# Rotary attention: where the two table products, the exchange of rows and the sum are made

## The chip, the cores and the metric

One core of a Trainium2 chip runs the whole program in one launch. The metric is the device time of one execution, in microseconds (us), as the median of three runs. The traces and pages are those of one profiled execution. Engines: TensorE (PE; PEld is its weight load), VectorE (DVE), ScalarE (ACT), GpSimd (POOL), SyncE (SP; SPq is its queue of DMA issues).

## The reference

The program is a chain of eight blocks over x of 8 x 512 x 256. Only the sixth is touched, a causal attention of 16 heads of 64 with rotary positions and four learned keys and values ahead of the tokens:

```python
def rotate_half(x):
    x1 = x[..., ::2]; x2 = x[..., 1::2]
    return jnp.stack((-x2, x1), axis=-1).reshape(x.shape)
def apply_rope(t):
    ...
    return t * cos + rotate_half(t) * sin
h = rms_norm(x, norm_weight)
q, k, v = jnp.split(h @ w_qkv.T, 3, axis=-1)        # then split into 16 heads
q = apply_rope(q); k = apply_rope(k)
k = jnp.concatenate([pm, k], axis=2); v = jnp.concatenate([pm, v], axis=2)
scores = jnp.einsum('bhid,bhjd->bhij', q, k) * scale
scores = jnp.where(causal, scores, jnp.finfo(scores.dtype).min)
out = jnp.einsum('bhij,bhjd->bhid', jax.nn.softmax(scores, axis=-1), v)
return out.transpose(0, 2, 1, 3).reshape(b, n, heads * dim_head) @ w_out.T
```

## The kernel before

`attention_core` serves two stages; with `rope` set it is the rotary attention, without it another block's attention (the `flat_` branches), which the diff leaves alone. Tensors lie with features on the partitions: a pair of heads fills 128 partitions, 512 tokens lie along a row. Values of 32 bits are split into a high and a low half of 16 bits, so that a product is three matmuls.

**Slots.** Work goes by a pair of heads n of a batch, 8 pairs and 8 batches. `slots` runs the slots -2, -1 and 0 once and then 64 slots in a loop of four turns of 16. In slot s each engine works on up to four pairs at once, in an order written out by hand in its `rope_slot`: the rotation of pair s+2, the scores and maxima of pair s+1, the transposed scores and exponentials of pair s, and the value products and outputs of pair s-1. Every eighth slot also projects a batch's outputs (`outputs`, line 915, and `add_outputs`, line 1028). Engines meet through semaphores only. A wait holds everything behind it on its engine, the queue of DMA issues included.

**The rotation.** Operation j is pair j//2, its queries when j is even and its keys when odd. All of them use one PSUM bank (`pj`), one pair of SBUF tiles (`ab`) and one tile for the sum (`rot`), so they go one after the other:

- TensorE's `project` (line 832) makes `pj`, once `evac` says that it is free.
- VectorE's `rotate` multiplies `pj` by the cosines into `ab[:,0]` (line 979) and copies `pj` with neighbouring partitions exchanged into `ab[:,1]` (line 980, STREAM_SHUFFLE). It first waits for the sum of the operation before.
- GpSimd's `turn` multiplies `ab[:,1]` by the signed sines (line 1138), and `sum_up` adds both into `rot` (line 1142).
- ScalarE's `high` casts `rot` to 16 bits into `QK` (line 1080), and GpSimd's `low` subtracts to get the low half (line 1147). The next sum waits for it.

**The order around it.** VectorE's slot: low weights of the second tile (`low_weights`, line 1007) and maxima of the third group (line 990); the split of the maxima; low weights of the third and fourth tile; rotate the queries; `normalise` (reciprocal, line 1019, which waits for the last value product, `pv_done`); `low_values` (line 1014); maxima of the first group; rotate the keys; maxima of the second group (lines 990, 991); `low_outputs` (line 1024); low weights of the first tile. TensorE's slot: project the queries; transposed scores 3 of pair s-1 (lines 881 to 888); value products (line 901), the last of which counts `pv_done`; transposed scores 0; scores of the first group (line 857); project the keys; turn the outputs; scores of the second group; transposed scores 1; scores of the third group, which wait for the maxima of the second; project values (line 838); transposed scores 2. ScalarE's slot: exponentials 2 and 3 of pair s-1 (lines 1088, 1093); cast of the keys of pair s+1; the turned maxima (line 1083); high values (line 1098); exponentials 0; copy of the outputs (line 1101); exponentials 1; cast of the queries of pair s+2. SyncE's slot, once each of 64: wait for this slot's last value product, then load 2 KB of value tails for a later pair (line 1064).

Of the kernel before, what the change touches and what calls it, by code (L numbers as in the profile page):

```python
# [5 lines left out]
P=128  # L6
# [754 lines left out]
def attention_core(nc, XT, HT, c_):  # L761
# [26 lines left out]
    with ExitStack() as ctx:  # L788
# [5 lines left out]
        QK=sb("QK",[P,4,2,2,PM+T],F16)  # L794
        ab=sb("ab",[P,2,T]) if rope else None
        rot=sb("rot",[P,1 if rope else 2,T])
        PH=sb("PH",[P,2,PCOLS],F16); PL=sb("PL",[P,2,PCOLS],F16); P32=sb("P32",[P,2,2,PM+T])
# [5 lines left out]
        mtp=s_ps[:,0,:].bitcast(BF16)  # L803
        h_hi,h_ready,cleared,proj,evac,turned,summed,hi,lo,pm_kept=[sem(n) for n in "h_hi,h_ready,cleared,proj,evac,turned,summed,hi,lo,pm_kept".split(",")]
        v_done,v_hi,v_low,o_low=[sem(n) for n in "v_done,v_hi,v_low,o_low".split(",")]
        tail_in=[sem(f"tail_in{i}") for i in range(4)] if rope else None
        s_done,maxed,m_step,m_ready,m_turned,m_copied=[sem(n) for n in "s_done,maxed,m_step,m_ready,m_turned,m_copied".split(",")]
# [5 lines left out]
        def batch(it,n): return (it*BPI+n//NP_)%NB  # L813
# [149 lines left out]
        def _(dve):  # L963
# [10 lines left out]
            def rotate(it,j):  # L974
                n,what=divmod(j,2)
                if rope:
                    if j: dve.wait_ge(summed,it*2*S+j)
                    dve.wait_ge(proj,it*2*S+j+1)
                    nc.vector.tensor_tensor(ab[:,0],pj[:,:],c_.tab[:,0],ALU.mult)
                    nc.vector.stream_shuffle(ab[:,1],pj[:,:],[i^1 for i in range(32)]).then_inc(evac,1)  # L980
                else:
# [76 lines left out]
        if rope:  # L1058
            @block.sync
            def _(sp):  # L1060
                sp.wait_ge(cleared,CL)
                def tail_rows(b,n):
                    rows=c_.tails[bass.ds(b,1),:,n%NP_].rearrange("a m part h d -> (a m) part h d")
                    sp.dma_start(V[0:PM,n%4,QT,:,:,0:DH],rows).then_inc(tail_in[n%4],16)
                for n in range(4): tail_rows(0,n)
                with loop(nc,sp,NB//BPI) as it:
                    for n in range(4,S+4):
                        sp.wait_ge(pv_done,it*S*QT+(n-3)*QT)
                        tail_rows(batch(it,n),n)
                for i in range(4): sp.wait_ge(tail_in[i],16*(NB*NP_//4+1))  # L1070
        else: c_.select(nc,block,ctx,hi)
        @block.scalar
        def _(act):
# [35 lines left out]
            def rope_slot(it,s):  # L1109
# [4 lines left out]
                if s>=-1: high_values(it,s+1)  # L1114
                if s>=0: exps(it,s,0)
                if s>=1: keep_outputs(it,s-1)
                if s>=0: exps(it,s,1)
                high(it,2*(s+2))
            def flat_slot(it,s):
# [15 lines left out]
        def _(pool):  # L1135
            def turn(it,j):
                pool.wait_ge(evac,it*2*S+j+1)
                nc.gpsimd.tensor_tensor(ab[:,1],ab[:,1],c_.tab[:,1],ALU.mult).then_inc(turned,1)  # L1138
            def sum_up(it,j):
                if j: pool.wait_ge(lo,it*2*S+j)  # L1140
                pool.wait_ge(turned,it*2*S+j+1)
                nc.gpsimd.tensor_tensor(rot_of(j),ab[:,0],ab[:,1],ALU.add).then_inc(summed,1)  # L1142
            def low(it,j):
# [10 lines left out]
            def rope_slot(it,s):  # L1154
                q,k=2*(s+2),2*(s+2)+1
                if s>=-1: low(it,2*(s+1)+1)
                turn(it,q); sum_up(it,q)
                if new_batch(s): low_tokens(it,s+3)
                turn(it,k)
                low(it,q)  # L1160
                sum_up(it,k)
# [112 lines left out]
def rope_table():  # L1274
# [3 lines left out]
    f=np.repeat(f,2,axis=-1).T  # L1278
    sign=np.where(np.arange(DH)%2==0,-1,1).astype(np.float32)[:,None]
    one=np.stack([np.cos(f),np.sin(f)*sign],1).astype(np.float32)  # L1280
# [986 lines left out]
```

## Time and profile before

| | |
|---|---|
| median of three runs | 3782.42 us (3779.88 to 3782.56) |
| profiled execution | 3805.44 us |
| its span, first to last instruction | 3803.5 us |
| attention core | from about 2081 to 3021 us of the span |
| busy over the span | PE 83%, DVE 59%, ACT 44%, POOL 32% |

The page cuts the span into 40 slices and gives each engine's busy share in tenths, and the TensorE clock that the throttle granted, in tenths of full speed. Attention fills slices 22 to 31 or so:

```profile
## 2 busy tenths in 40 slices
PE   8677488988889889689985899999999889999571
...
DVE  4667644444444444478865888889888745555233
ACT  2179333333333333366743555556555534444230
POOL 0032410000000000133311655566555544443342
PEclk9899755555555555599997999999999955555786
DMA  4011110000000000011001000000000010110335
```

Times in the rows below are in us from the span's start unless marked ns. "[0.34 <-POOL att_rot L1142]" behind a row of a timeline says that the engine was idle for 0.34 us ahead of it and what ended that. The rows are of the profiled execution; a term taken from them is set against its time, 3805.4 us.

### The profile page before, as it was taken

Reading aid. Unit: us, or ns where it says so; the run is one execution under the profiler, and the core shown is the slowest. Engines: PE = TensorE matmul, PEld = TensorE weight load, DVE = VectorE, ACT = ScalarE, POOL = GpSimd, SP = SyncE. Lnnn points to the kernel's source line nnn. Section 1 sums busy time; section 2 is a strip of 40 time slices with the busy share of each in tenths; the row PEclk is TensorE's granted clock in tenths of the full one; section 3 lists DMA queues with packets and bytes.
Section 4 is the critical chain, followed back from the end, with each engine's and each line's share of the span. In section 5 each row is a group of like instructions: output and inputs, shape, how many; then the busy total and the mean of one; then the engine's idle time right before and its main releaser. Section 6 shows DMA issues by size and latency. Waiting matters only on the chain. (4 is left out here: it accounts for less than half of the span.)

```text
span 3803.5 us, 143700 instructions
## 1 busy us (share of the span) xinstructions
PE 3140.8 (83%) x58958; PEld 2400.2 (63%) x58958; DVE 2247.7 (59%) x6777; ACT 1692.0 (44%) x5164; POOL 1216.8 (32%) x1533
## 2 busy tenths in 40 slices
PE   8677488988889889689985899999999889999571
PEld 5545278888888888545532666666666567777451
DVE  4667644444444444478865888889888745555233
ACT  2179333333333333366743555556555534444230
POOL 0032410000000000133311655566555544443342
PEclk9899755555555555599997999999999955555786
DMA  4011110000000000011001000000000010110335
GB/s 133 1 55 46 31 26 14 14 25 14 25 14 14 25 14 25 15 33 25 17 1 52 2 2 3 2 3 3 2 3 2 16 51 30 32 33 28 109 102 173
DMA packets 110725, 116.07 MB, mean 31 GB/s; under 512 B 52782, under 2 KB 94199, under 8 KB 110112
## 3 DMA queue, kind: packets, MB, share of 16 engines
q1 hardware_dynamic: 102416, 87.33, 8.1%
q0 software_dynamic: 7824, 21.46, 1.6%
q8 instruction: 403, 6.60, 0.7%
q14 instruction: 82, 0.67, 0.1%
HBM read 79.62 MB, written 29.13 MB: 29 GB/s over the span
## 5 line engine op out<-in xcount | busy, mean ns | idle before, releaser
L676 PE MATMUL banks<-hp,whp 128*128 128x8 f16 x24576 | 741.6, 168 | 117.5 <-DVE hp L743 117.5
L676 PEld LDWEIGHTS banks<-hp,whp 128*128 128x128 f16 x24576 | 698.0, 104 | 178.2 <-DVE hp L743 169.4
L709 ACT ACTIVATE ig<-banks 128x32 f32<-128x32 f32 x512 | 100.9, 197 | 577.2 <-PE banks L676 577.2
L738 DVE SCALAR_TENSOR_TENSOR carry<-ig 128x16 f32<-128x16 f32 x512 | 91.6, 179 | 424.9 <-ACT ig L709 424.9
L646 POOL COPY HT<-hist 128x128 f32 x64 | 21.2, 407 | 986.6 <-DVE hp L748 986.6
L1088 ACT ACTIVATE att_PH<-att_stp 128x1024 f16<-128x1024 f32 (+3 forms) x258 | 183.2, 710 | 325.4 <-PE att_stp L888 325.4
L1753 PE MATMUL rnn_banks<-rnn_hp,rnn_whp 128*128 128x8 f16 x6144 | 285.4, 171 | 40.3 <-ACT rnn_hp L1811 15.4
L1753 PEld LDWEIGHTS rnn_banks<-rnn_hp,rnn_whp 128*128 128x128 f16 x6144 | 248.3, 107 | 107.1 <-ACT rnn_hp L1811 76.1
L1007 DVE TENSOR_TENSOR att_PL<-att_P,att_PH 128x1024 f16<-128x1024 f32 (+3 forms) x257 | 266.3, 1075 | 0.5 <-issue 0.2
L654 PE MATMUL banks<-xs,wxp 128*128 128x64 f16 x3168 | 263.7, 241 | 0.0
L1147 POOL TENSOR_TENSOR att_QK<-att_rot,att_QK 128x512 f16<-128x512 f32 x133 | 174.2, 1310 | 239.6 <-ACT att_QK L1080 239.6
L1905 DVE TENSOR_TENSOR rnn_hp<-rnn_hist,rnn_hp 128x16 f16<-128x16 f32 x512 | 97.7, 191 | 227.6 <-ACT rnn_hist L1812 218.7
L1811 ACT ACTIVATE rnn_hp<-rnn_banks 128x16 f16<-128x16 f32 x512 | 93.7, 183 | 279.5 <-PE rnn_banks L1753 277.4
L832 PE MATMUL att_pj<-att_hT,att_w 128*128 128x512 f16 x804 | 201.0, 386 | 17.4 <-POOL att_hT L1151 15.6
L990 DVE TENSOR_REDUCE att_mx<-att_sp 128x2 f32<-128x264 f32 (+3 forms) x263 | 209.6, 818 | 1.1 <-PE att_sp L862 1.1
L1138 POOL TENSOR_TENSOR att_ab<-att_ab,att_rope 128x512 f32<-128x512 f32 x134 | 169.8, 1267 | 124.2 <-DVE att_ab L980 123.4
L1142 POOL TENSOR_TENSOR att_rot<-att_ab 128x512 f32<-128x512 f32 x134 | 204.2, 1524 | 14.8
L654 PEld LDWEIGHTS banks<-xs,wxp 128*128 128x128 f16 x3168 | 194.5, 126 | 0.0
L1093 ACT ACTIVATE att_P<-att_stp 128x1024 f32<-128x1024 f32 (+3 forms) x258 | 180.6, 700 | 5.3 <-DVE att_PL L1007 5.3
L901 PE MATMUL att_acc<-att_V,att_PH 128*128 128x65 f16 (+1 forms) x3584 | 180.0, 193 | 0.0
L743 DVE TENSOR_TENSOR hp<-og,tc 128x16 f16<-128x16 f32 x512 | 90.1, 176 | 144.2 <-ACT tc L715 144.2
L901 PE MATMUL att_acc<-att_V,att_PL 128*128 128x65 f16 x1792 | 175.0, 192 | 0.0
(606 smaller groups left out, 7712.9 us busy)
## 6 DMA issues: line engine op xcount, KB each, us to landing
gen_w<-in_L_cond_W_dram SPq DMA_DIRECT2D x32, 512.0 KB
exp_xt<-expert_rows_scratch SPq DMA_DIRECT2D x80, 129.0 KB
edge_cb<-cols_scratch SPq DMA_DIRECT2D x16, 512.0 KB, 3.8
XT<-expert_found_scratch SPq DMA_DIRECT2D x16, 512.0 KB, 4.9
mod_xn<-in_x_dram SPq DMA_DIRECT2D x8, 512.0 KB
XT<-in_xT_dram SPq DMA_DIRECT2D x1, 4096.0 KB
out_dram<-exp_ob SPq DMA_DIRECT2D x64, 64.0 KB, 2.2
attw_st<-in_L_attn_w_qkvT_dram SPq DMA_DIRECT2D x6, 512.0 KB
```

What stands on the lines that cost most here:

```text
L654: last=nc.tensor.matmul(out, wxp[:,wpart,k,col:col+128], xs[:,st,xpart,k,steps], start=False,stop=False,skip_group_check=True)
L676: last=nc.tensor.matmul(out, whp[:,wpart,k,col:col+128], hp[:,k,hpart], start=False,stop=True,skip_group_check=True)
L832: last=nc.tensor.matmul(pj[:,:],c_.w_of(n)[:,wpart,k,col:col+P],h_of(n)[:,xpart,k,PM:PM+T],start=(i==0),stop=(i==5)); i+=1
L901: last=nc.tensor.matmul(out[:,0:wide],p[:,h,at:at+P],V[:,n%4,tt,part,h,0:wide],start=(tt==0 and a==0 and p is PH and part==0),stop=(tt==(R ...
L990: i=nc.vector.tensor_reduce(out=mx[:,:,qt:qt+1],in_=s_ps[:,:,at:at+w_],axis=X_AX,op=ALU.max); at+=w_
L1007: i=nc.vector.tensor_tensor(PL[:,:,at:at+w_],P32[:,t%2,:,0:w_],PH[:,:,at:at+w_],ALU.subtract)
L1088: nc.scalar.activation(PH[:,:,at:at+w_],st_ps[:,:,0:w_],ACT.Exp,scale=DH**-0.5)
L1093: i=nc.scalar.activation(P32[:,t%2,:,0:w_],st_ps[:,:,0:w_],ACT.Exp,scale=DH**-0.5)
L1138: nc.gpsimd.tensor_tensor(ab[:,1],ab[:,1],c_.tab[:,1],ALU.mult).then_inc(turned,1)
L1142: nc.gpsimd.tensor_tensor(rot_of(j),ab[:,0],ab[:,1],ALU.add).then_inc(summed,1)
L1147: nc.gpsimd.tensor_tensor(dst[:,1],rot_of(j),dst[:,0],ALU.subtract).then_inc(lo,1)
L1753: last=nc.tensor.matmul(pre(st,par)[:,u,j], whp[:,wpart,k,u*P:u*P+P], hp[:,k,hpart], start=False,stop=True,skip_group_check=True)
```

## The change

The exchange of neighbouring rows moves behind the product with the sines. VectorE makes both products from `pj`; in the second, the row's own sine is used with the sign of the row that it will go to (the table's signs are flipped). Two DMAs on SyncE's queue, one for the odd and one for the even rows, copy `ab[:,1]` into a new tile `swapped` with neighbours exchanged, 64 rows of 2 KB each. GpSimd's `turn` goes, and its `sum_up` waits for both DMAs. SyncE's slot becomes: the wait for the last value product and the tail load as before, then the swap of the queries, then that of the keys. ScalarE casts the queries ahead of the outputs' copy and of exponentials 1, in place of behind them. GpSimd's order is otherwise kept.

```diff
@@ attention_core
+        swapped=sb("swapped",[P,T]) if rope else None
...
+        swapped_in=sem("swapped_in")
@@ VectorE, rotate
                     nc.vector.tensor_tensor(ab[:,0],pj[:,:],c_.tab[:,0],ALU.mult)
-                    nc.vector.stream_shuffle(ab[:,1],pj[:,:],[i^1 for i in range(32)]).then_inc(evac,1)
+                    nc.vector.tensor_tensor(ab[:,1],pj[:,:],c_.tab[:,1],ALU.mult).then_inc(evac,1)
@@ SyncE
+                def swap_rows(it,j):
+                    sp.wait_ge(evac,it*2*S+j+1)
+                    for r in range(2): sp.dma_start(swapped[r::2,:],ab[1-r::2,1]).then_inc(swapped_in,16)
+                def rope_slot(it,s):
+                    if s>=1:
+                        sp.wait_ge(pv_done,it*S*QT+s*QT)
+                        tail_rows(batch(it,s+3),s+3)
+                    swap_rows(it,2*(s+2))
+                    swap_rows(it,2*(s+2)+1)
                 for n in range(4): tail_rows(0,n)
-                with loop(nc,sp,NB//BPI) as it:
-                    for n in range(4,S+4):
-                        sp.wait_ge(pv_done,it*S*QT+(n-3)*QT)
-                        tail_rows(batch(it,n),n)
+                slots(rope_slot,sp)
@@ ScalarE, rope_slot
                 if s>=0: exps(it,s,0)
+                high(it,2*(s+2))
                 if s>=1: keep_outputs(it,s-1)
                 if s>=0: exps(it,s,1)
-                high(it,2*(s+2))
@@ GpSimd
-            def turn(it,j):
-                pool.wait_ge(evac,it*2*S+j+1)
-                nc.gpsimd.tensor_tensor(ab[:,1],ab[:,1],c_.tab[:,1],ALU.mult).then_inc(turned,1)
             def sum_up(it,j):
                 if j: pool.wait_ge(lo,it*2*S+j)
-                pool.wait_ge(turned,it*2*S+j+1)
-                nc.gpsimd.tensor_tensor(rot_of(j),ab[:,0],ab[:,1],ALU.add).then_inc(summed,1)
+                pool.wait_ge(swapped_in,32*(it*2*S+j+1))
+                nc.gpsimd.tensor_tensor(rot_of(j),ab[:,0],swapped[:,:],ALU.add).then_inc(summed,1)
@@ GpSimd, rope_slot
-                turn(it,q); sum_up(it,q)
+                sum_up(it,q)
                 if new_batch(s): low_tokens(it,s+3)
-                turn(it,k)
                 low(it,q)
                 sum_up(it,k)
@@ rope_table
-    sign=np.where(np.arange(DH)%2==0,-1,1).astype(np.float32)[:,None]
+    sign=np.where(np.arange(DH)%2==0,1,-1).astype(np.float32)[:,None]
```

## Rows read from the trace of the kernel before

**Rows 1.** Windows view, one ordinary slot; columns as the first row names them:
```profile
...
core 0: us, PE busy (x) PEld busy (x) DVE busy (x) ACT busy (x) POOL busy (x), PEclk, DMA share, GB/s
...
2602.90:2615.80 12.90, 11.92 (x221) 8.44 (x218) 12.24 (x24) 8.14 (x17) 8.18 (x7) 1.00 0.01 3
...
```

**Rows 2.** Waits of VectorE from 2100 to 3000 us: us in total, times, longest:
```profile
...
DVE att_inv L1019 <- PE att_acc L901: 12.5, 42, 0.3
DVE att_ab L979 <- PE att_pj L832: 10.5, 35, 2.6
DVE att_ab L979 <- POOL att_rot L1142: 9.6, 21, 0.8
...
```

**Rows 3.** Timeline of VectorE: start us, us, engine, line, op, out<-in, [idle before]:
```profile
...
2500.79 0.72 DVE L980 STREAM_SHUFFLE att_ab<-att_pj 128x512 f32<-128x512 f32 x1
2501.58 0.21 DVE L1019 RECIPROCAL att_inv<-att_acc 128x8 f32<-128x8 f32 x1
...
2504.40 0.69 DVE L979 TENSOR_TENSOR att_ab<-att_pj,att_rope 128x512 f32<-128x512 f32 x1 [0.34 <-POOL att_rot L1142]
...
2506.50 0.16 DVE L991 TENSOR_REDUCE att_mx<-att_sp 128x2 f32<-128x8 f32 x1
...
2512.96 0.67 DVE L979 TENSOR_TENSOR att_ab<-att_pj,att_rope 128x512 f32<-128x512 f32 x1
...
2514.60 0.21 DVE L1019 RECIPROCAL att_inv<-att_acc 128x8 f32<-128x8 f32 x1 [0.30 <-PE att_acc L901]
...
2517.32 0.69 DVE L979 TENSOR_TENSOR att_ab<-att_pj,att_rope 128x512 f32<-128x512 f32 x1
...
```

**Rows 4.** Timeline of TensorE, from the key rotation of one slot to the next:
```profile
...
2506.72 0.39 PE L857 MATMUL att_sp<-att_QK 64*128 64x512 f16 x2 [0.94 <-DVE att_mx L991]
...
2515.81 1.47 PE L832 MATMUL att_pj<-att_hT,att_w 128*128 128x512 f16 x6
...
```

**Rows 5.** Timeline of GpSimd, the sums of queries and of keys in one slot:
```profile
...
2503.01 1.27 POOL L1142 TENSOR_TENSOR att_rot<-att_ab 128x512 f32<-128x512 f32 x1
...
2509.48 1.87 POOL L1142 TENSOR_TENSOR att_rot<-att_ab 128x512 f32<-128x512 f32 x1
...
```

**Rows 6.** Groups by shape, 2100 to 3000 us: xcount, busy us, mean ns, idle before:
```profile
...
L1138 POOL TENSOR_TENSOR att_ab<-att_ab,att_rope 128x512 f32<-128x512 f32 x126 | 159.7, 1267 | 113.4 <-DVE att_ab L980 112.6
L1007 DVE TENSOR_TENSOR att_PL<-att_P,att_PH 128x776 f16<-128x776 f32 x63 | 114.2, 1813 | 0.5 <-issue 0.2
...
L980 DVE STREAM_SHUFFLE att_ab<-att_pj 128x512 f32<-128x512 f32 x127 | 92.2, 726 | 0.0
L979 DVE TENSOR_TENSOR att_ab<-att_pj,att_rope 128x512 f32<-128x512 f32 x127 | 86.6, 682 | 20.2 <-PE att_pj L832 10.5 <-POOL att_rot L1142 9.6
...
```

**Rows 7.** Timeline of the SyncE queue, the tail load of the slot at 2500 us:
```profile
...
2501.71 0.26 SPq L1064 DMA_DIRECT2D att_V<-value_tails_scratch  x1
```

**Rows 8.** The instructions of line 1064: duration ns min/median/max:
```profile
...
L1064 SPq DMA_DIRECT2D att_V<-value_tails_scratch x68: 254/255/301, 2075.0 to 3013.5; - x68
L1064 SPq FUSED_REGOPS  x64: 37/37/101, 2117.5 to 3013.4; - x64
L1064 SPq MOVE att_V<-value_tails_scratch x64: 29/29/29, 2117.6 to 3013.5; - x64
...
```

**Rows 9.** The stores of line 2010, 64 KB each: issue, and issue to landing:
```profile
...
L2010 SPq DMA_DIRECT2D out_dram<-exp_ob x64: 315/426/510, 3756.2 to 3800.3; - x64
...
DMA to landing us min/median/max: 1.9/2.2/4.2
```

**Rows 10.** The page, DMA issues: count, KB each, median us to landing:
```profile
...
XT<-expert_found_scratch SPq DMA_DIRECT2D x16, 512.0 KB, 4.9
...
```

**Rows 11.** Timeline of ScalarE, the first and second tile's exponentials:
```profile
...
2503.53 1.02 ACT L1093 ACTIVATE att_P<-att_stp 128x1024 f32<-128x1024 f32 x1
...
2505.83 0.82 ACT L1088 ACTIVATE att_PH<-att_stp 128x776 f16<-128x776 f32 x1 [0.50 <-PE att_stp L888]
...
```

**Rows 12.** Timeline of VectorE in a batch slot, behind the output products:
```profile
...
2456.68 0.96 DVE L1007 TENSOR_TENSOR att_PL<-att_P,att_PH 128x776 f16<-128x776 f32 x1
...
```

More of the change, by code:

```diff
@@ L803, in attention_core @@
         mtp=s_ps[:,0,:].bitcast(BF16)
-        h_hi,h_ready,cleared,proj,evac,turned,summed,hi,lo,pm_kept=[sem(n) for n in "h_hi,h_ready,cleared,proj,evac,turned,summed,hi,lo,pm_kept".split(",")]
+        h_hi,h_ready,cleared,proj,evac,summed,hi,lo,pm_kept=[sem(n) for n in "h_hi,h_ready,cleared,proj,evac,summed,hi,lo,pm_kept".split(",")]
         v_done,v_hi,v_low,o_low=[sem(n) for n in "v_done,v_hi,v_low,o_low".split(",")]
+        swapped_in=sem("swapped_in")
         tail_in=[sem(f"tail_in{i}") for i in range(4)] if rope else None
```

## The prediction

> **What bounds the kernel now.** I went from the stage to the loop inside it. The attention stage repeats one slot per pair of heads: 64 in the loop, 56 ordinary ones and eight that also project a batch's outputs. The windows view of one ordinary slot, 12.90 us long, has TensorE busy 11.92 us and VectorE 12.24 us at a granted clock of 1.00, the 2.4 GHz level [rows 1]. Both look full, so busy shares don't say which is the bound; the waits do. In 42 of 62 slots VectorE's reciprocal waits for the last value product of TensorE, and its rotation of the keys (line 979, second use in a slot) waits 35 times for TensorE's projection and 21 times for GpSimd's sum [rows 2]. So VectorE has slack in most slots, 0.3 us at one place and 0.2 us at the other, and TensorE doesn't.
>
> The two timelines give the loop. VectorE begins the keys' rotation at 2504.40 and ends the maxima of the second group at 2506.66, that is 2.26 us later [rows 3]. TensorE, which had waited 0.94 us for exactly this, starts the third group's scores at 2506.72 [rows 4]. It works through the slot's list until the last value product, which releases the reciprocal at 2514.60, 7.94 us after the maxima [rows 3]. Then it makes the next transposed scores, the first scores and the keys' projection, which ends at 2515.81 + 1.47 = 2517.28 [rows 4], and the next rotation of the keys starts at 2517.32, 2.72 us after the reciprocal [rows 3]. 2.26 + 7.94 + 2.72 = 12.92 us is the slot. A delay between the reciprocal and the keys' rotation is paid in full; work taken off VectorE elsewhere isn't.
>
> In that last piece a second chain runs beside TensorE: query products, GpSimd's turn, GpSimd's sum, key rotation. It is just long enough to show. In the slot at 2500 the queries' shuffle ends at 2501.51, the sum at 2503.01 + 1.27 = 2504.28, and the keys' rotation starts at 2504.40, after 0.34 us of waiting [rows 3, 5]; the piece is 2.82 us there. Over the stage the piece is about 2.77 us. This second chain is what the change touches.
>
> **The change part by part.** *VectorE.* The shuffle (726 ns) becomes a product with one PSUM and one SBUF operand, as line 979 is (682 ns) [rows 6]. In the loop this is 0.04 us per slot, 64 x 0.04 = 2.8 us gained.
>
> *GpSimd* loses its turns, 1.27 us each, one before each sum [rows 6]. Of its remaining work only the queries' sum, 1.27 us, stands on the chain [rows 5].
>
> *SyncE and DMA.* Each rotation now issues two DMAs of 64 rows of 2 KB. For the queries SyncE comes to them only behind this slot's wait for the last value product and the load of value tails: the program has that wait first. In the next slot the queries' rotation starts at 2512.96 and its two operations of 0.7 us are done by 2514.3, while the value product releases the reciprocal only at 2514.60 [rows 3]: the products are ready, and the queue isn't. Working from the reciprocal's start (2501.58), SyncE begins the tail load at +0.13 and has issued it at +0.39 [rows 3, 7]. Its register work before an issue is 37 + 29 ns [rows 8], so the first swap is issued at +0.46.
>
> The time from the first issue to the landing of both has no row of its own. The second issue follows by one issue's length: 0.26 us for the tail load [rows 8], 0.43 for a 64 KB store [rows 9]; I take 0.3, nearer the first, since the swap's rows are as plain as a load's. For the landing the nearest row is the 64 KB store of 64 rows, 1.9 us at least, 2.2 in the median, 4.2 at most [rows 9]. Those are issued eight in a row onto each other's heels, while attention's DMA share is 0.01 [rows 1], so I take its least, 1.9. That makes 2.2 us from first issue to both landed. The bounds: 1.3 us, if a landing into SBUF takes half of that store's; and, on the line from 64 KB in 2.2 us to 512 KB in 4.9 us [rows 10], 3.35 us for the 256 KB of both.
>
> The Trainium skill, "DMA: Bandwidth & Descriptors", section on the anatomy of one DMA, puts a DMA at about 2.0 us fixed plus bytes over 436 GB/s. For 128 KB that is an estimate of 2.3 us in place of 1.9, and by it the sum below would be 26 us longer. It adds that the wait is mostly the target memory's receipt, HBM's being the heaviest, which speaks for less with SBUF as the target; no row here shows an SBUF to SBUF transfer.
>
> Then GpSimd wakes (0.10, estimated by VectorE's 0.12 after GpSimd), sums (1.27), and VectorE starts 0.12 later: 0.46 + 2.2 + 0.10 + 1.27 + 0.12 = 4.15 us from the reciprocal to the keys' rotation, in place of 2.77. **+1.38 us per slot.** The batch slots have the same piece, and behind it TensorE's output products wait for VectorE as the scores do, so I count all 64 slots, once each, as the tail load's 64 register steps count them [rows 8]: 64 x 1.38 = 88 us.
>
> For the keys, SyncE is free: it issues right behind the products, at +1.4 us from the rotation's start, the rows land at +3.6, and the sum is made by +5.3 even if GpSimd first waits for a subtraction of VectorE's. The next to ask for it is the next slot's query rotation, which started at 2512.96, 8.6 us after the keys' at 2504.40 [rows 3]. So it costs nothing; were SyncE 3 us late, it would begin to.
>
> *ScalarE.* The queries' cast moves ahead of the outputs' copy and the second exponentials. ScalarE ends the first tile at 2504.55, +2.97, and the sum is there at +4.0: it stands idle for a microsecond, and the second exponentials, which began at 2505.83, +4.25, begin about as much later [rows 11]. That delays no one, since TensorE's use of them, in the transposed scores behind the third group's, has itself moved by 1.38. If that cover were gone, a good microsecond could stand on the loop instead.
>
> *Prologue.* Six rotations ahead of the loop have the transfer in series too, at most 0.9 us each (2.2 for a turn of 1.27); I take 3 us, which cancels VectorE's gain of 2.8.
>
> **Sum:** +88 us. The profiled execution took 3805.4 us and the median of the three runs is 3782.4, 0.6% less; the difference is not in this stage's terms, so I add 88 to either: 3893 for a profiled one, **3870 for the median**.
>
> **Rivals.** *A short swap.* Landing 1.3 us after the first issue: the piece is 3.25 us, +0.48 per slot, +31: 3813 us. For it: a quiet DMA system, a target in SBUF. Against: no row below 1.9.
>
> *A long swap.* At 3.35 us (two transfers behind each other) +2.53 per slot, +162: 3944 us. For: 4.9 us for 512 KB. Against: those are large loads issued together.
>
> *Not slower: the swap is hidden and VectorE gets its time back.* The place is the lock-step of the key sum and the subtraction of line 1007. The 128x776 subtraction takes 1813 ns in the mean beside GpSimd [rows 6], and 0.96 us in a batch slot [rows 12]; GpSimd's sum takes 1.87 us there in place of 1.27 [rows 5]. So 0.85 us per ordinary slot is lost on VectorE to GpSimd. If VectorE were the bound and the sum came after the subtraction, 56 x 0.85 = 48 us would be won: 3735 us. It decides only if the swap lands within 0.8 us of its issue (4.15 - 2.2 + 0.8 = 2.75), and even then TensorE holds the slot at 12.9, which leaves about 5 us: 3777, no change. The Trainium skill, "SBUF — State Buffer", section on its two sides, states this lock for a VectorE operation with two SBUF inputs against a GpSimd one that reads SBUF, and that the first to start makes the other wait; the rows agree.
>
> *The clock.* TensorE's busy share falls from 92% to some 84%. If a tenth of the slots fell to the 1.2 GHz level, about 6 x 11.9 = 71 us would come on top: 3941. Nothing in this stage's rows shows it.
>
> **Chances.** My forecast (swap of 1.9 to 2.7 us, 3850 to 3902) 0.75; short swap 0.10; long swap 0.08; clock 0.03; hidden swap 0.04, half of it faster and half no change. The range reaches 3815 at the short swap and 3920 toward the long one; outside are the hidden one, half of the short, most of the long and the clock, near 0.2. This kernel's measurement can tell 0.2% (7.6 us) from no change: faster 0.02, within 0.02, slower 0.96.
>
> **What would show it.** In the changed profile: slots near 14.3 us; the keys' rotation waiting 1.3 us or more for GpSimd's sum in nearly every slot and never for the projection; TensorE's wait ahead of the third group's scores up from 0.94 to about 2.3 us; the first swap issued right behind each tail load, not right behind the queries' products; ScalarE idle ahead of the queries' cast. I am wrong if the swaps are issued ahead of the tail load's wait, if they land within 0.8 us, or if the slot stays at 12.9.

## The result, and the profile after

The changed kernel takes 3977.9 us (median of 4 runs, 3973.7 to 3979.2) against 3781.2 us (4 runs): ratio 1.052, interval 1.050 to 1.0537, or 197 us slower. The forecast was 3870, range 3815 to 3920: the sign was right, the size less than half. The profiled execution's span is 3976.2 us, where the kernel before had 3803.5.

VectorE's timeline of the changed kernel, two slots in a row, answers to [rows 3] (line 1021 is the reciprocal, 981 the rotation's first product, 993 the end of a group's maxima):

```profile
2542.40 0.18 DVE L1021 RECIPROCAL att_inv<-att_acc 128x8 f32<-128x8 f32 x1
...
2546.78 0.69 DVE L981 TENSOR_TENSOR att_ab<-att_pj,att_rope 128x512 f32<-128x512 f32 x1 [1.93 <-POOL att_rot L1147]
...
2548.86 0.16 DVE L993 TENSOR_REDUCE att_mx<-att_sp 128x2 f32<-128x8 f32 x1
...
2558.50 0.21 DVE L1021 RECIPROCAL att_inv<-att_acc 128x8 f32<-128x8 f32 x1 [0.37 <-PE att_acc L903]
...
2563.07 0.69 DVE L981 TENSOR_TENSOR att_ab<-att_pj,att_rope 128x512 f32<-128x512 f32 x1 [2.09 <-POOL att_rot L1147]
...
2565.15 0.16 DVE L993 TENSOR_REDUCE att_mx<-att_sp 128x2 f32<-128x8 f32 x1
...
2573.24 0.21 DVE L1021 RECIPROCAL att_inv<-att_acc 128x8 f32<-128x8 f32 x1 [0.37 <-PE att_acc L903]
```

Reciprocal to the keys' rotation takes 4.38 and 4.57 us, where it took 2.82. And the stretch that the forecast left alone, from the end of the second maxima to the next reciprocal, takes 2573.24 - 2565.31 = 7.93 us in the second slot, as before, but 2558.50 - 2549.02 = 9.48 us in the first. The windows view over that first slot says why (columns as in [rows 1]; the seventh figure, behind POOL's, is the granted clock):

```profile
2544.00:2546.00 2.00, 2.00 (x25) 1.21 (x24) 0.86 (x2) 1.18 (x2) 0.61 (x1) 1.00 0.28 105
2546.00:2548.00 2.00, 0.41 (x10) 0.19 (x4) 1.22 (x3) 1.30 (x3) 1.26 (x2) 1.00 0.00 0
2548.00:2550.00 2.00, 0.77 (x12) 0.54 (x12) 2.00 (x5) 1.22 (x2) 0.56 (x1) 1.00 0.23 88
2550.00:2552.00 2.00, 2.00 (x22) 1.83 (x20) 2.00 (x3) 0.00 (x0) 1.22 (x1) 0.59 0.14 51
2552.00:2554.00 2.00, 2.00 (x19) 1.04 (x17) 1.30 (x4) 0.53 (x2) 0.74 (x1) 0.56 0.00 0
2554.00:2556.00 2.00, 2.00 (x43) 1.25 (x42) 0.70 (x1) 0.93 (x5) 0.00 (x0) 1.00 0.00 0
```

TensorE is busy for 0.41 and 0.77 of 2.00 us in two windows, and in the next two its clock is 0.59 and 0.56: most of that time is at 1.2 GHz. TensorE's timeline around it, to be held against [rows 4]:

```profile
2549.08 0.39 PE L859 MATMUL att_sp<-att_QK 64*128 64x512 f16 x2 [2.66 <-DVE att_mx L993]
...
2550.27 2.07 PE L840 MATMUL att_vo<-att_w,att_hT 128*128 128x128 f16 x18
```

The wait ahead of the third group's scores is 2.66 us, where it was 0.94. The 18 products of line 840 behind it take 2.07 us; in a slot of the same run in which the clock doesn't fall they take 1.18:

```profile
2320.34 1.18 PE L840 MATMUL att_vo<-att_w,att_hT 128*128 128x128 f16 x18
```

The queues show the new chain. SyncE's and GpSimd's timelines from 2558 us on (compare [rows 5, 7]):

```profile
2558.64 0.26 SPq L1066 DMA_DIRECT2D att_V<-value_tails_scratch  x1
2559.01 1.11 SPq L1069 DMA_DIRECT2D att_swapped<-att_ab  x2
```

```profile
2561.68 1.27 POOL L1147 TENSOR_TENSOR att_rot<-att_ab,att_swapped 128x512 f32<-128x512 f32 x1 [3.41 <-DMA att_swapped<-att_ab]
```

The swap's first issue stands 0.51 us behind the reciprocal, the sum 2561.68 - 2559.01 = 2.67 us behind that, and the rotation 1.39 us later: 4.57. Over the 56 ordinary slots the means are 0.48 us to the first issue, 0.52 from there to the second, 2.25 from the second to the sum's start (2.16 in the median; in five slots it is 2.75 or more, four of them with a second issue of 1.2 us or more), and 1.39 to the rotation. The instructions of the swap, from 2110 to 3190 us (ns min/median/max):

```profile
L1069 SPq DMA_DIRECT2D att_swapped<-att_ab x252: 464/536/1647, 2111.6 to 3189.4; - x126
```

The waits of the same stretch (us in total, times, longest), of TensorE, VectorE, ScalarE and SyncE's queue, for [rows 2]:

```profile
PE att_sp L859 <- DVE att_mx L993: 152.2, 56, 3.8
PE att_vo L917 <- DVE att_ao L1026: 25.0, 7, 3.9
...
DVE att_ab L981 <- POOL att_rot L1147: 134.3, 63, 3.0
...
DVE att_inv L1021 <- PE att_acc L903: 19.5, 53, 0.5
DVE att_ab L981 <- PE att_pj L834: 2.8, 1, 2.8
...
ACT att_QK L1088 <- POOL att_rot L1147: 100.5, 63, 2.6
...
SPq L1066 <- PE att_acc L903: 624.6, 62, 20.2
SPq L1069 <- DVE att_ab L982: 272.7, 64, 7.5
```

VectorE waits for the sum in all 63 slots, 2.13 us each, and for the projection once. And by shape, for [rows 6], VectorE's subtraction and GpSimd's sum (xcount, busy us, mean ns, idle before):

```profile
L1009 DVE TENSOR_TENSOR att_PL<-att_P,att_PH 128x776 f16<-128x776 f32 x62 | 68.0, 1096 | 0.5 <-issue 0.2
...
L1147 POOL TENSOR_TENSOR att_rot<-att_ab,att_swapped 128x512 f32<-128x512 f32 x125 | 189.7, 1517 | 365.8 <-DMA att_swapped<-att_ab 365.8
```

**The account.** One table serves all kernels: from the timelines, the means over the 56 ordinary slots of A, reciprocal to the keys' rotation; B, reciprocal to the end of the second maxima; C, from there to the next reciprocal; and the slot, B + C. Then the granted clock from 2200 to 3000 us and the number of stretches at 1.2 GHz in the trace's clock records (3.4 or 6.8 us long) among the loop's slots.

| kernel | us, median | ratio (95%) | A | B | C | slot | clock | stretches |
|---|---|---|---|---|---|---|---|---|
| before | 3781.2 | 1 | 2.78 | 5.04 | 7.93 | 12.98 | 1.00 | 0 |
| after | 3977.9 | 1.052 (1.050-1.054) | 4.62 | 6.86 | 9.11 | 15.96 | 0.92 | 46 |
| e1_fill | 3910.5 | 1.035 (1.033-1.037) | 4.62 | 6.85 | 8.15 | 15.01 | 0.99 | 3 |
| e2_swap_first | 3907.8 | 1.035 (1.033-1.036) | 3.99 | 6.23 | 8.69 | 14.92 | 0.95 | 27 |
| e7_two_queues | 3917.5 | 1.037 (1.035-1.039) | 4.10 | 6.34 | 8.70 | 15.03 | 0.96 | 30 |
| e6_cast_back | 3976.9 | 1.052 (1.050-1.054) | 4.61 | 6.84 | 9.15 | 16.00 | 0.92 | 47 |
| e3_one_more | 3952.6 | 1.046 (1.044-1.047) | 4.09 | 6.35 | 9.37 | 15.72 | 0.93 | 44 |
| e5_delay_fill | 3960.9 | 1.049 (1.047-1.051) | 4.32 | 6.58 | 9.43 | 16.01 | 1.00 | 0 |
| e10_vector_delay | 3962.2 | 1.049 (1.047-1.051) | 4.26 | 6.52 | 9.40 | 15.91 | 0.93 | 46 |
| e11_vector_delay_fill | 3973.2 | 1.051 (1.049-1.053) | 4.43 | 6.69 | 9.49 | 16.18 | 1.00 | 0 |
| e14_between_delay | 3958.3 | 1.048 (1.046-1.050) | 4.38 | 6.62 | 8.79 | 15.41 | 0.94 | 36 |
| e15_between_delay_fill | 3895.0 | 1.031 (1.030-1.033) | 4.47 | 6.70 | 8.01 | 14.72 | 1.00 | 3 |
| e4_keys_last | 3813.1 | 1.009 (1.007-1.010) | 4.99 | 4.40 | 9.49 | 13.89 | 1.00 | 3 |
| e8_queries_first | 3815.5 | 1.010 (1.009-1.012) | 2.76 | 4.99 | 8.66 | 13.65 | 1.00 | 1 |
| e9_queries_first_keys_last | 3887.6 | 1.030 (1.028-1.031) | 5.33 | 4.81 | 10.24 | 15.05 | 0.97 | 16 |
| e12_queries_between | 3811.7 | 1.008 (1.007-1.010) | 2.95 | 5.19 | 8.22 | 13.41 | 0.98 | 9 |
| e13_between_fill | 3832.2 | 1.014 (1.013-1.016) | 3.05 | 5.29 | 8.57 | 13.86 | 1.00 | 0 |
| e16_between_keys_last | 3855.8 | 1.020 (1.018-1.022) | 5.35 | 4.83 | 9.67 | 14.50 | 0.98 | 11 |

Ratios are against the kernel before on the same chip (medians of 3777.3 to 3781.2 us). Of after against before, B grew by 1.82 us in 56 slots and by 2.14 in the seven batch slots between the loop's reciprocals: 117 us. C grew by 1.18 us in 56 and by 1.66 (19.14 to 20.80) in seven: 78 us. Together 195, of 197.

The slots of one run can also be told apart by whether C has such a stretch in it. In the changed kernel 39 of the 56 ordinary slots have one, and there C takes 9.57 us in the mean; of the other 17, 15 take 7.93, as in the kernel before. All seven batch slots have one.

### The profile page after: what moved, and what is told of

It reads as the page before. It is cut to its first block and busy times, and to the rows that moved or that the text cites. A ratio compares the mean times of both kernels' runs of the same rounds, so it can differ in the third digit from the quotient of the medians.

```text
span 3976.2 us, 143700 instructions
## 1 busy us (share of the span) xinstructions
PE 3221.7 (81%) x58958; PEld 2444.9 (61%) x58958; DVE 2210.1 (56%) x6643; ACT 1684.5 (42%) x5164; POOL 1025.2 (26%) x1399
## 5 line engine op out<-in xcount | busy, mean ns | idle before, releaser
L1147 POOL TENSOR_TENSOR att_rot<-att_ab,att_swapped 128x512 f32<-128x512 f32 x134 | 202.4, 1511 | 394.3 <-DMA att_swapped<-att_ab 394.3
L1009 DVE TENSOR_TENSOR att_PL<-att_P,att_PH 128x1024 f16<-128x1024 f32 (+3 forms) x257 | 223.5, 890 | 99.0 <-ACT att_P L1102 61.1
L1152 POOL TENSOR_TENSOR att_QK<-att_rot,att_QK 128x512 f16<-128x512 f32 x133 | 154.8, 1164 | 373.3 <-ACT att_QK L1088 373.3
L834 PE MATMUL att_pj<-att_hT,att_w 128*128 128x512 f16 x804 | 214.2, 406 | 19.5 <-POOL att_hT L1156 15.8
L859 PE MATMUL att_sp<-att_QK 64*128 64x132 f16 (+3 forms) x528 | 75.5, 309 | 161.8 <-DVE att_mx L993 159.3
L981 DVE TENSOR_TENSOR att_ab<-att_pj,att_rope 128x512 f32<-128x512 f32 x134 | 91.4, 682 | 159.4 <-POOL att_rot L1147 150.5
```

The lines of the kernel that those rows point to most:

```text
L834: last=nc.tensor.matmul(pj[:,:],c_.w_of(n)[:,wpart,k,col:col+P],h_of(n)[:,xpart,k,PM:PM+T],start=(i==0),stop=(i==5)); i+=1
L1009: i=nc.vector.tensor_tensor(PL[:,:,at:at+w_],P32[:,t%2,:,0:w_],PH[:,:,at:at+w_],ALU.subtract)
L1147: nc.gpsimd.tensor_tensor(rot_of(j),ab[:,0],swapped[:,:],ALU.add).then_inc(summed,1)
L1152: nc.gpsimd.tensor_tensor(dst[:,1],rot_of(j),dst[:,0],ALU.subtract).then_inc(lo,1)
```

## Experiments: is the second loss TensorE's clock?

Theory CLOCK: the longer wait of TensorE in each slot lets its granted clock fall, and C grows by that alone. Rival: the transfers disturb TensorE or ScalarE, and the clock only goes with it.

**e1_fill.** Eight products of 512 columns into a bank that is free just then, results unused, where TensorE would wait:

```diff
                 if s>=0: scores_T(it,s,1)
+                if s>=1: fill()
+    def fill():
+        for i in range(8): nc.tensor.matmul(acc[:,0,:],c_.w_of(0)[:,0,0,0:P],c_.w_of(0)[:,0,0,0:512],...)
```

> The changed kernel with eight products of 512 columns more on TensorE in each slot, ahead of the third group's scores, where it waits; they write a PSUM bank that is free there and nobody reads them. Theory CLOCK (the wait of 2.66 us ahead of these scores lets TensorE's granted clock fall to 1.2 GHz, which costs 1.17 us in an ordinary slot and 1.64 in a batch slot): the clock of the stage goes from 0.92 to about 1.00, maxima to reciprocal from 9.1 back to 7.9 us, the time from 3978 to about 3899 us. Theory TRAFFIC (TensorE is slow there because the keys' swap moves 256 KB through SBUF at the same time): maxima to reciprocal stays near 9.1 us, the time near 3978. Either way reciprocal to keys' rotation stays 4.6 us.

Measured: 3910.5 us, 67 us less than the changed kernel, with A unchanged. The windows view from 2200 to 3000 us, of the changed kernel and then of this one:

```profile
2200.00:3000.00 800.00, 664.25 (x10131) 444.25 (x10129) 536.72 (x969) 371.96 (x742) 255.27 (x192) 0.92 0.09 32
```

```profile
2200.00:3000.00 800.00, 737.92 (x11100) 474.62 (x11101) 576.15 (x1035) 397.47 (x787) 275.05 (x208) 0.99 0.09 35
```

The DMA share is the same 0.09, the clock 0.99, and C falls from 9.11 to 8.15: TensorE was given more work, and the kernel became faster. So the transfers don't lengthen C by themselves.

**e3_one_more.** The kernel before, with one more GpSimd operation of the sum's length in the queries' chain and no DMA:

```diff
 pool.wait_ge(turned,it*2*S+j+1)
+if j%2==0:
+    nc.gpsimd.tensor_tensor(spare[:,:],ab[:,0],ab[:,1],ALU.add).then_inc(spared,1)
+    pool.wait_ge(spared,it*S+j//2+1)
```

> The kernel before, without any swap, with one more GpSimd operation of 1.27 us between the queries' turn and their sum, its result unused. The keys' rotation comes 1.35 us later, about as my forecast had it for the change: reciprocal to keys' rotation about 4.15 us. Theory CLOCK: the clock falls in part of the slots though no transfer is there; maxima to reciprocal over 7.93 us in the mean, time 3890 to 3950. Theory TRAFFIC: clock 1.00, 7.93 us, time 3781 + 64 x 1.38 = 3869.

Measured: 3952.6 us; the windows view:

```profile
2200.00:3000.00 800.00, 673.01 (x10280) 451.68 (x10281) 629.65 (x1087) 385.71 (x753) 456.36 (x339) 0.93 0.01 2
```

The delay of A is 1.31 us, worth 84 us in 64 slots; the loss is 174, a little over the theory's range, and the clock falls with a DMA share of 0.01. But the fall isn't what costs the rest: C takes 9.40 us in the 39 ordinary slots with a stretch at 1.2 GHz and 9.31 in the 17 without. Only in five batch slots does it cost, 20.5 us for 19.2, some 7 us in all. VectorE's groups by shape show what does, since GpSimd is busy for longer and locks with VectorE's subtractions:

```profile
L1009 DVE TENSOR_TENSOR att_PL<-att_P,att_PH 128x1024 f16<-128x1024 f32 x53 | 103.1, 1945 | 0.0
L1009 DVE TENSOR_TENSOR att_PL<-att_P,att_PH 128x776 f16<-128x776 f32 x53 | 100.2, 1890 | 0.5 <-issue 0.2
```

The first of these took 1258 ns before. **e5_delay_fill** is this kernel with e1's products:

> The kernel before with the one GpSimd operation more of e3_one_more and the eight TensorE products of e1_fill (neither result is used). Theory CLOCK: what e3_one_more cost beyond its delay was the clock; with TensorE fed in the gap the clock is 1.00 and maxima to reciprocal 7.93 to 8.15 us, and what is left is the delay alone, 64 x 1.32 = 84 us, with some 10 us for the products themselves: 3865 to 3875 us, which is what my forecast's sum would have had for a delay of this size. Rival (the loss in e3_one_more was the longer lock between GpSimd and VectorE): near 3950.

Measured: clock 1.00, no stretch at 1.2 GHz, and still C = 9.43 and 3960.9 us. The rival won: with the clock back, VectorE holds C at the same length, since its two long subtractions still take over 3.8 us together, and that of 128x264 grew to 1185 ns.

**e10_vector_delay, e11_vector_delay_fill.** So the delay was made on VectorE, in the kernel before, without GpSimd and without a DMA; e11 has the eight products too.

```diff
 dve.wait_ge(proj,it*2*S+j+1)
+if j%2:
+    for i in range(2):
+        nc.vector.tensor_tensor(spare[:,:],pj[:,:],c_.tab[:,0],ALU.mult).then_inc(spared,1)
+        dve.wait_ge(spared,2*(it*S+j//2)+i+1)
 nc.vector.tensor_tensor(ab[:,0],pj[:,:],c_.tab[:,0],ALU.mult)
```

> The kernel before with two extra VectorE products (one operand from PSUM, 64 queries wide, results unused) ahead of the keys' rotation in each slot: a delay of the loop without a DMA and without a further GpSimd operation. Expected from it: the piece from the reciprocal to the keys' rotation grows from 2.78 us to 4.0 to 4.1. Theory that TensorE's longer wait in each slot lowers its granted clock, and that this costs time by itself: mean granted clock of the stage below 0.97, dozens of stretches at 1.2 GHz, and the time well over the bare delay of 64 x 1.3 = 84 us: 3890 to 3950. Rival, that only the delay counts and the clock was the transfers' or GpSimd's doing: clock 1.00 and 3863 +-10.

> The same delay with eight TensorE products of 512 columns, results unused, ahead of the third group's scores. Clock theory: granted clock back at 1.00, the piece from the second maxima to the next reciprocal back at 7.9 to 8.2 us, and 3863 to 3880 us. Rival, that the products only take TensorE's time: clock as in the run without them, and a time at or above that run's.

Measured: e10 has clock 0.93, 46 stretches and 3962.2 us, 88 more than its delay of 1.48 us explains (95); e11 has clock 1.00 and 3973.2. The clock does as the theory says, the time of e11 as its rival does. Hardly any of the 88 us is the clock's: in e10 C takes 9.37 us in the 44 ordinary slots with a fall and 9.50 in the 12 without; two batch slots lose 1.6 us each. Waits of VectorE and TensorE in e11:

```profile
DVE att_inv L1028 <- PE att_acc L903: 1.6, 1, 1.6
...
PE att_acc L903 <- DVE att_PL L1019: 36.2, 54, 0.7
```

VectorE no longer waits for the last value product (once, where it was 42 times before), and TensorE's value products wait for VectorE 54 times. The kernel before has no room on VectorE: [rows 2] gave 0.3 us in 42 of 62 slots, and the moved slot lets GpSimd's keys' operations meet more subtractions (that of 128x1024 takes 1998 ns here). In this kernel a delay can't be had alone.

**e14_between_delay, e15_between_delay_fill.** The pair once more on e12_queries_between (below), where VectorE waits 1.3 us per slot for TensorE's last value product:

> The same kernel with two extra VectorE products ahead of the keys' rotation, which put it off by 1.2 to 1.5 us; VectorE waits 1.3 us per slot for TensorE elsewhere, so it has the room. The bare delay is worth 64 x 1.4 = 90 us, from 3812 to about 3900. Clock theory: more stretches at 1.2 GHz (30 or more), second maxima to reciprocal up from 8.22 to 8.8 or more, time 3925 to 3970. Rival, that the clock was never the cost: 8.2 us stays, 3900 +-10.

> That delay with the eight extra TensorE products. Clock theory: granted clock 1.00, second maxima to reciprocal at 8.0 to 8.2 us, and a time below that of the run without the products by 30 us or more, 3880 to 3905. Rival, that VectorE or something else holds the slot: the time stays within 10 us of the run without the products, with the clock at 1.00.

Measured: 3958.3 and 3895.0 us. The products bring 63 us (44 of them are C's 8.79 - 8.01 = 0.78 us in 56 slots, 12 C's in the batch slots), while VectorE still has its slack (72.8 and 73.1 us of waiting for the value product, in 52 and 55 slots). e14's windows view and e15's:

```profile
2200.00:3000.00 800.00, 669.45 (x10392) 448.01 (x10389) 608.21 (x1095) 387.91 (x762) 267.21 (x199) 0.94 0.09 33
```

```profile
2200.00:3000.00 800.00, 751.23 (x11338) 483.64 (x11335) 637.21 (x1154) 411.10 (x805) 285.87 (x212) 1.00 0.10 35
```

This is the clean pair: the same delay, the same transfers, room on VectorE, and 63 us, 56 of which stand in C. Within e14 C is 9.48 us in the 31 ordinary slots with a fall and 7.93 in each of the 25 without. The Trainium skill, "TensorE: Matmul & The Clock Gate", section Terms, prices a lowered clock at the time spent at it times the share of pulses left out, a half here. By that the difference of the two, 133 - 10 us at 1.2 GHz, is an estimate of 61 us, and the changed kernel's 174 us one of 87 against its 78 in C. The runs come near both.

## Experiments: the transfer and its place

**e2_swap_first.** The queries' swap issued ahead of SyncE's wait for the last value product and the tail load:

```diff
+swap_rows(it,2*(s+2))
 if s>=1:
     sp.wait_ge(pv_done,it*S*QT+s*QT)
     tail_rows(batch(it,s+3),s+3)
-swap_rows(it,2*(s+2))
```

> The changed kernel with SyncE issuing the queries' swap ahead of its wait for the last value product and of the tail load. Theory QUEUE (the swap is held 0.4 to 0.8 us by what is ahead of it on SyncE): first swap issued within 0.1 us of the queries' products, reciprocal to keys' rotation from 4.6 to about 3.9 us, 64 x 0.7 = 45 us less, 3933; with the clock of theory CLOCK coming back in part, down to 3860. Rival (the transfer alone sets the piece): stays at 4.6 us and 3978.

Measured: A 3.99 us, 0.63 less, and 3907.8 us, 70 less. 40 us of that are A's 64 x 0.63; the rest is C's, with 27 stretches for 46. So the queue's order costs 0.63 us, more than the time from the reciprocal to the first issue (0.48), since the products are ready before the reciprocal: the first issue now stands 0.25 us ahead of it in the mean. A stays 1.2 us too long even with a queue that is free.

**e7_two_queues.** The second DMA of each swap is issued by ScalarE:

```diff
-for r in range(2): sp.dma_start(swapped[r::2,:],ab[1-r::2,1]).then_inc(swapped_in,16)
+sp.dma_start(swapped[0::2,:],ab[1::2,1]).then_inc(swapped_in,16)       # SyncE
+act.dma_start(swapped[1::2,:],ab[0::2,1]).then_inc(swapped_in,16)      # ScalarE, ahead of exps(it,s,0)
```

> The changed kernel with the swap's second DMA issued by ScalarE, ahead of its first exponentials for the queries and behind its second ones for the keys, in place of SyncE. Theory ISSUE (one issue of 64 rows takes 0.47 to 0.59 us, and the second one's length is part of the swap): first SyncE issue to sum from 2.67 to about 2.1 us, reciprocal to keys' rotation from 4.6 to 4.1 us, 30 us from that and up to 40 from the clock, 3910 to 3950. Rival (both DMAs share the same engines and the transfer itself sets the landing): 2.67 and 4.6 us stay, 3978.

Measured: A 4.10, 3917.5 us. The lengths of the issues, and those of the changed kernel's over the same stretch:

```profile
L1069 SPq DMA_DIRECT2D att_swapped<-att_ab x110: 464/465/487, 2110.2 to 2993.3; - x110
L1119 ACTq DMA_DIRECT2D att_swapped<-att_ab x110: 472/496/505, 2110.2 to 2993.3; - x110
```

```profile
L1069 SPq DMA_DIRECT2D att_swapped<-att_ab x206: 464/536/1647, 2111.6 to 2996.3; - x103
```

With the issues side by side A shrinks by 0.52 us, the time from one issue to the next in the changed kernel, and from SyncE's issue to the sum's start are 2.24 us for 2.76. That is the term I had at 0.3.

**e6_cast_back.** ScalarE's cast of the queries is put back behind the second exponentials:

> The changed kernel with ScalarE's cast of the queries put back behind the second exponentials, as in the kernel before. If ScalarE's order is off the loop, the time is the changed kernel's, 3978 +-10 us, and the segments of the slot stay at 4.6, 6.9 and 9.1 us. If the moved cast is part of the loss, the time falls by 20 us or more.

Measured: 3976.9 us and the same segments. The moved cast is neither part of the loss nor of any use in this order; that part of the forecast stands.

## Experiments: is there an order in which the change pays?

All have e2's edit, and differ in where VectorE rotates. **e8_queries_first** has the queries' rotation ahead of the subtractions of tiles 3 and 4, **e12_queries_between** has it between them (and ScalarE's cast behind the outputs' copy):

```diff
-if s>=1: low_weights(it,s-1,2); low_weights(it,s-1,3)
+if s>=1: low_weights(it,s-1,2)
 rotate(it,2*(s+2))
+if s>=1: low_weights(it,s-1,3)
```

> The changed kernel with SyncE issuing the queries' swap first (as e2_swap_first) and VectorE rotating the queries ahead of the subtractions of the third and fourth tile. The queries' products are ready 1.1 us or more before the reciprocal, so the sum is there about 2.9 us behind it and TensorE's projection (2.7 us) nearly hides it: slot 13.1 us, clock 1.00, no wait of TensorE over 1.5 us; time 3790 to 3810. Rival (the two subtractions, now later, hold TensorE's value products): reciprocal late by up to 1 us, 3850.

> The changed kernel with the queries' swap issued ahead of SyncE's other waits, VectorE's rotation of the queries between the subtractions of tiles 3 and 4, and ScalarE's cast behind the outputs' copy. Theory, that the change's loss is the place of the sums in the loop and not the swap as such: piece 2.8 to 2.9 us, second maxima to next reciprocal 8.1 to 8.3, slot 13.1 to 13.3, time 3785 to 3805. Rival, that two engines' locked operations on one port give the gain back: slot at 13.6 or more, time 3815 or more.

Measured: 3815.5 and 3811.7 us. In both A is back or nearly so, at 2.76 and 2.95, and the transfer hidden. What is left stands mostly in C. e8's time is outside its theory's range, and what its rival named is there, at a smaller price. In e8 TensorE's value products wait for a subtraction that has moved behind the rotation:

```profile
PE att_acc L903 <- DVE att_PL L1012: 22.8, 48, 0.6
PE att_acc L903 <- DVE att_PL L1009: 8.0, 6, 1.5
```

In e12 that is 8.7 us in 11 slots, and 9 stretches at 1.2 GHz remain. Neither theory had e12's time: its slot of 13.41 us is between the theory's 13.3 and the rival's 13.6. **e13_between_fill**, e12 with the eight products, was to show that the rest is the clock's:

> The kernel with the queries' rotation between the subtractions of tiles 3 and 4 (segments 2.95, 5.19, 8.22 us, slot 13.41, 9 stretches at 1.2 GHz), with the eight extra TensorE products ahead of the third group's scores. Theory, that half of what it still loses to the kernel before is the clock: no stretch at 1.2 GHz, second maxima to reciprocal 8.0 to 8.15 us, time 3792 to 3806. Rival, that its loss is the order's own: 3808 or more.

Measured: 3832.2 us, 20 more. The rival's number came, but it doesn't say that the order itself costs it: TensorE waited 54.7 us in 53 slots in e12, 1.03 us each, and the eight products take 1.90 us from first to last in e1's timeline, so here they stood on the loop themselves:

```profile
2568.43 1.90 PE L921 MATMUL att_acc<-att_w 128*128 128x512 f16 x8
```

So this run doesn't say how much of e12's last 32 us is the clock's, but e12's own slots do: C takes 9.45 us in the eight ordinary ones with a fall and 7.93 in 43 of the 48 without. With the one batch slot that has a fall (21.66 us for 20.2 at most in the other six) that makes some 14 us; the rest is the order's.

**e4_keys_last** puts the second maxima and the outputs' low half ahead of the keys' rotation, **e9_queries_first_keys_last** adds e8's edit, **e16_between_keys_last** e12's:

```diff
-rotate(it,2*(s+2)+1)
 if s>=-1: maxima(it,s+1,1)
 if s>=1: low_outputs(it,s-1)
+rotate(it,2*(s+2)+1)
```

> The changed kernel with three orders changed: SyncE issues the queries' swap ahead of the tail load's wait; VectorE takes the maxima of the second group and the outputs' low half ahead of the keys' rotation; ScalarE casts the queries behind the outputs' copy. The late sum is then off TensorE's loop. Theory LOOP (the slot is TensorE's list plus what VectorE does between the reciprocal and the second maxima): slot about 12.6 us, clock 1.00, the 128x776 subtraction near 0.96 us, time about 3760. Rival (VectorE, now waiting about 1 us for the second group's scores, becomes the bound): slot 13.2 us or more, 3800 or more.

> e4_keys_last (slot 13.9 us) with VectorE also rotating the queries ahead of the subtractions of the third and fourth tile, so that GpSimd's key sum runs beside a rotation, which has one SBUF operand, and not beside a subtraction, which has two. Theory LOCK (in e4_keys_last the sum only moved on to block the 128x520 subtraction for 1.05 us): the two subtractions together back to 1.05 us, slot about 13.0 us, time 3770 to 3790. Rival (TensorE's value products then wait for the subtractions): slot stays 13.5 or more, 3800 or more.

> The queries' rotation between the subtractions of tiles 3 and 4, and the second maxima and the outputs' low half ahead of the keys' rotation. If the queries' sum is then ready in time and the keys' sum meets no long subtraction, TensorE no longer waits 0.9 us for the second maxima and the slot falls below 12.98 us: 3700 to 3775. Rival, by what the two orders with late keys showed: the keys' sum moves on to the subtractions, the next slot's value products wait for VectorE, slot 13.5 to 15, 3810 to 3890. I hold the rival for likelier.

Measured: 3813.1, 3887.6 and 3855.8 us, in all three the rival's range. B falls below the kernel before's (4.40 to 4.83 for 5.04), but C takes 9.5 to 10.2 us. Waits of TensorE and VectorE in e4, from 2110 to 3000 us:

```profile
PE att_acc L903 <- DVE att_PL L1012: 31.7, 51, 0.7
PE att_sp L859 <- DVE att_mx L993: 21.2, 52, 0.4
```

```profile
DVE att_mx L992 <- PE att_sp L868: 49.9, 59, 1.6
```

TensorE's wait ahead of the third scores is down to 0.4 us, and its clock at 1.00; now VectorE waits for scores and TensorE for subtractions, in turn. No kernel here is faster than the one before; the nearest are e12 and e4, 0.8 and 0.9% above it.

## Why the prediction was right and wrong

**The loop and the sign: right.** A delay between the reciprocal and the keys' rotation is paid in full. B grew by as much as A (1.82 and 1.84), and where A went back, in e8 and e12, most of the loss went with it.

**The chain of the queries: right in its order, short in two terms.** SyncE issues the swap behind the tail load, VectorE waits for the sum in every slot, ScalarE idles for 1.6 us ahead of the cast. The piece was to be 4.15 us and is 4.62. The means are, against the sum's terms: 0.48 us to the first issue for 0.46; 0.52 from the first issue to the second for 0.3; 2.25 from the second issue to the sum's start for 1.9 + 0.10; 1.39 to the rotation, as reckoned. So two terms are short by about a quarter of a microsecond each. One is the second issue, which I priced by the tail load, "since the swap's rows are as plain as a load's": an issue of this swap takes 0.46 us at least and 0.54 in the median, more than the 64 KB store's 0.43, and e7 gave 0.52 us back by setting the two beside each other. The other is the landing: I took the store's least, 1.9 us, and its median, 2.2, was nearer. The page of e14 gives the swap's DMA 2.1 us from issue to landing (count, KB each, median us):

```profile
att_swapped<-att_ab SPq DMA_DIRECT2D x268, 128.0 KB, 2.1
```

The Trainium skill's figure for one DMA of this size, weighed in the prediction ("DMA: Bandwidth & Descriptors", section on the anatomy of one DMA), was 2.3 us, which is more than the 2.1; the page gives it for DMAs that GpSimd issues, and these are SyncE's. The two terms make 64 x 0.47 = 30 of the 108 us that I missed.

**The clock: the failed step.** I wrote "Nothing in this stage's rows shows it" and gave it a chance of 0.03 and a tenth of the slots. It fell 46 times in the 63 slots between the loop's reciprocals and took 78 us. The sum has no term for it: it took a longer wait of TensorE to cost its own length and nothing behind it. The row that spoke against that stood in my own argument: TensorE's one wait per slot, 0.94 us, was to become 2.3 us. The busy share came out at 83% from 2200 to 3000 us, where I had 84, and the clock at 0.92 all the same. What the changed kernel's stage shows: each of the 46 falls begins within 2.0 us behind the end of a wait of TensorE of 2.6 us or more, or, in five cases, inside it; 17 of the 63 such waits have none; and with part of the wait filled there are 3 falls (e1, 0.98 us left in the mean, and e15, 0.78). The length of one wait isn't all that counts: in e3 18 of the 44 falls come at waits of 2.04 to 2.12 us, and e4's three at two waits of 0.74 and 0.66 us that follow each other within 2 us. What decides whether a given wait brings a fall stays open. The rival's price was wrong in both factors: I reckoned 11.9 us for each slot that fell, where one costs 78/46 = 1.7 us, and 6 such slots, where 46 fell. That its 71 us lies near the measured 78 is luck.

**The lock of VectorE and GpSimd: right, and off the loop.** The 128x776 subtraction fell from 1813 to 1096 ns, as the turn no longer met it. I had priced that at nothing, since VectorE isn't the bound, and it brought nothing in the changed kernel: where the clock doesn't fall, C is 7.93 us as before. e5 and e11 show its other side: the kernel before has so little room on VectorE that a delay of 1.3 to 1.5 us makes the lock's cost the bound.

**SyncE's wait, the keys' swap, the prologue and the cast:** nothing in the account is left for them (195 of 197 us are B's and C's), and e6 shows it for the cast.

## What to carry to other kernels

Where a change lengthens TensorE's wait in a loop that keeps it nearly full, price the clock with the wait: here 1.8 us more per slot cost 117 us, and the clock another 78. A transfer put in the place of an engine's copy has to be issued as soon as its operands are made and well ahead of whoever waits for its result; the same change lost 197 us in one order and 32 in another. And a filler on TensorE pays where it fits into the wait and TensorE holds the loop: it brought 67 and 63 us where the wait was 2.5 to 2.7 us in the mean; it cost 20 where it was 1.0, and 8 and 11 where VectorE held the loop (e5, e11), though it brought the clock back there too. To see what a low clock costs, hold slots with a fall against slots without one in the same trace.

## What the runs showed of the hardware

- An issue of 64 rows of 2 KB from SBUF to SBUF holds SyncE for 0.46 us at least, 0.54 in the median and up to 1.65 (ScalarE 0.47 to 0.51), and two in a row on one queue are ready for use 2.68 us after the first begins (median; mean 2.76).
- In a stage with TensorE busy for over 80%, the granted clock can average 0.92: 46 stretches of 3.4 or 6.8 us at 1.2 GHz, in or right behind waits of 2.6 us and more. In e12, where the mean wait is 1.0 us, the falls come behind waits of 1.5 to 2.5 us. In the kernel before, with waits of 0.94 us in ordinary slots and 1.4 in batch slots, there is none.
- TensorE products that nobody uses make a kernel faster, by 1.6 to 1.7%, where they fill such a wait and TensorE holds the loop (e1, e15).
- A delay of 1.3 to 1.5 us per slot on VectorE or GpSimd, without any DMA, lowers the clock as the transfers' delay does (0.93 for 0.92). In these two kernels the ordinary slots with a fall are as long as those without, since VectorE holds them (C 9.40 and 9.31 us in e3, 9.37 and 9.50 in e10).
